# Score products of a local-attention block: 32 of 128 rows with zero-padded queries in place of 64 row-tile ones, and Exp's table loaded at another place

## What is computed

```
def local_attention(q, k, v):              # 16 heads of 64, windows of 32
    bk2, bv2 = (look(bk), look(bv))        # own window and the one before
    sim = jnp.einsum('bhwie,bhwje->bhwij', bq, bk2) * QK_SCALE
    sim = jnp.where(mask, -jnp.finfo(sim.dtype).max, sim)
    attn = jax.nn.softmax(sim, -1)
    out = jnp.einsum('bhwij,bhwje->bhwie', attn, bv2)

for i in range(6):
    x = attn_layer(shift_tokens(x), ...) + x     # q, k: l2norm, scale, rotary
    x = ffn_layer(shift_tokens(x), ...) + x      # layernorm, a * gelu(gate)

x = x + 0.5 * stack(layernorm(x))
x = x + recurrence(layernorm(x))
x = x + 0.5 * stack(layernorm(x))
```

## Time and profile before

| | |
|---|---|
| median of 3 runs | 3353.95 us (3350.72 to 3357.08) |
| the profiled execution | 3356.96 us, span 3355.2 us |
| granted TensorE clock | 0.996 of full speed |
| busy | PE 97%, PEld 74%, DVE 82%, ACT 76%, POOL 66% |
| steps | 192 tiles, one row maximum (L997) each |

### The profile page before, as it was taken

The page is one execution under the profiler, slowest core; times in us unless marked ns, Lnnn a source line. Parts: engine busy times, 40 slices in busy tenths (PEclk is TensorE's granted clock), DMA queues, the critical chain, the costliest instruction groups (busy, mean ns, idle before and its releaser), DMA issues. The chain is left out here.

```text
span 3355.2 us, 150147 instructions
## 1 busy us (share of the span) xinstructions
PE 3267.4 (97%) x63272; PEld 2487.9 (74%) x63464; DVE 2756.8 (82%) x6951; ACT 2542.9 (76%) x4144; POOL 2225.8 (66%) x1453
## 2 busy tenths in 40 slices
PE   7999999999999999999999999999999999999998
PEld 4777777777777777777777777777777777777776
DVE  7888888888878888889999888788888888888885
ACT  3777777777777777777777777777777777777775
POOL 6666666666666666667887666666666666666663
PEclk9999999999999999999999999999999999999999
DMA  3111111111111111111111111111111111111111
GB/s 122 44 47 44 47 44 47 44 46 44 40 47 44 47 44 47 44 47 45 38 47 43 48 44 45 41 44 47 44 47 44 47 44 44 44 41 47 47 52 38
DMA packets 135089, 157.39 MB, mean 47 GB/s; under 512 B 75539, under 2 KB 108439, under 8 KB 134423
## 3 DMA queue, kind: packets, MB, share of 16 engines
q1 hardware_dynamic: 129815, 144.42, 15.6%
q10 hardware_dynamic: 4608, 3.34, 0.3%
HBM read 33.38 MB, written 1.05 MB: 10 GB/s over the span
## 5 line engine op out<-in xcount | busy, mean ns | idle before, releaser
L1073 POOL TENSOR_TENSOR rot<-rot,swp 128x1024 f32<-128x1024 f32 x384 | 906.6, 2361 | 133.8 <-DVE rot L866 133.8
L673 ACT ACTIVATE sq<-proj 128x512 f32<-128x512 f32 x768 | 437.7, 596 | 459.5 <-PE proj L482 448.9
L482 PE MATMUL proj<-wq,xsT 128*128 128x512 f32 x1536 | 768.7, 622 | 14.3 <-DVE rot L866 11.1
L1082 POOL TENSOR_TENSOR rot<-rot,rn 128x1024 f32<-128x1024 f32 x384 | 724.1, 1907 | 0.0
L1063 POOL TENSOR_TENSOR rt<-rt,half 128x1 f32<-128x1 f32 x192 | 105.3, 548 | 797.4 <-DVE rt L936 797.4
L860 DVE TENSOR_TENSOR swp<-proj,tab 128x512 f32<-128x512 f32 x768 | 521.1, 679 | 5.7 <-ACT sq L673 3.6
L866 DVE TENSOR_TENSOR rot<-proj,tab 128x512 f32<-128x512 f32 x768 | 517.6, 674 | 0.6 <-PE tps L493 0.6
L493 PEld LDWEIGHTS tps<-idf,rot 128*128 128x128 f32 x3072 | 359.7, 141 | 204.3 <-issue 202.5
L990 DVE SCALAR_TENSOR_TENSOR hT<-proj,cols,fg 114x128 f32<-114x128 f32 (+1 forms) x576 | 166.7, 345 | 416.9 <-ACT fg L739 412.8
L1067 POOL TENSOR_TENSOR prob<-prob,rr 128x1024 f32<-128x1024 f32 x192 | 365.4, 1903 | 175.3 <-DVE rr L948 175.3
L525 PEld LDWEIGHTS sps<-kT,qT 64*32 64x32 f32 x24576 | 365.4, 107 | 130.0 <-issue 129.6
(11 more groups left out here) (102 smaller groups left out, 5872.1 us busy)
## 6 DMA issues: line engine op xcount, KB each, us to landing
vb<-va SPq DMA_DIRECT2D x192, 384.0 KB, 3.5
vb<-va SPq DMA_DIRECT2D x192, 128.0 KB, 3.6
wq<-in_L_ffn_Wqkv SPq DMA_DIRECT2D x95, 192.0 KB, 3.4
xs<-Z SPq DMA_DIRECT2D x192, 32.0 KB
wo<-in_L_ffn_Wo SPq DMA_DIRECT2D x94, 64.0 KB, 2.8
xs<-Z SPq DMA_DIRECT2D x192, 28.0 KB
xs<-Z SPq DMA_DIRECT2D x192, 3.8 KB
xs<-Z SPq DMA_DIRECT2D x192, 0.2 KB
```

The source lines that it names most:

```text
L482: mm(proj[:, c % 2, :], xsT[:, k.parity(L_QKV), 0:P], wq2[:, bass.ds(w + c * 512, 512)], start=True, stop=True).then_inc(p_qkv[c], 1)
L673: fn(sq[:, c * 512:(c + 1) * 512], proj[:, c % 2, :], ACT.Square).then_inc(a_sq[c], 1)
L1073: g_.tensor_tensor(r, r, swp[:, g * INNER:(g + 1) * INNER], ALU.add).then_inc(g_add[g], 1)
L1082: g_.tensor_tensor(r, r, rn[:, g * HEADS:(g + 1) * HEADS].unsqueeze(2) .to_broadcast([P, HEADS, DH]), ALU.mult).then_inc(g_nm[g], 1)
```

## The change

The queries get zeros. `qT` becomes, for each head pair and each of the 4 windows of the tile, two blocks of 32 columns: in block hp only the 64 rows of head hp hold queries, the other 64 rows are zero (set once by a memset on VectorE at the start). One product with all 128 rows, 64 columns of weights (two heads of 32 queries) and 64 moving columns of `kT` (both heads' keys on the rows) gives both heads' scores, since the zeros cancel the other head's keys. So there is one product where there were two, 32 in place of 64, and consecutive ones write to the other half of the output partitions (g).

The copy into `qT` becomes two, one for each head's 64 rows, since each goes to its own block. And ScalarE gets at the end of its step, after the xsT copies, an Exp on one column whose result `spare` nobody reads; the compiler's table load for Exp goes ahead of it, and Exp itself has none any more.

```
-        qT = sb("qT", [PAIRS, P])
+        qT = sb("qT", [PAIRS, POS // 2, 2, WIN])
...
+        spare = sb("spare", [1])
...
                 for p in range(PAIRS):
-                    for g in range(2):
-                        for hp, ty in ((0, 0), (1, 1), (0, 1), (1, 0)):
+                    for ty in range(2):
+                        for g in range(2):
                             w = 2 * ty + g
                             at = par * P + w * WIN
-                            rows = slice(hp * DH, (hp + 1) * DH)
-                            to = g * 64 + hp * WIN
-                            last = mm(sps[to:to + WIN, ty, p * 64:p * 64 + 64], qT[rows, p, w * WIN:(w + 1) * WIN],
-                                      kT[rows, p, at:at + 2 * WIN], start=False, stop=True, skip_group_check=True)
+                            last = mm(sps[g * 64:(g + 1) * 64, ty, p * 64:p * 64 + 64], qT[:, p, w, :, :].rearrange("p h i -> p (h i)"),
+                                      kT[:, p, at:at + 2 * WIN], start=False, stop=True, skip_group_check=True)
...
-                    cp(qT[:, :, :], tps[:, :, :]).then_inc(a_qT, 1)
+                    for hp in range(2):
+                        rows = slice(hp * DH, (hp + 1) * DH)
+                        last = cp(qT[rows, :, :, hp, :], tps[rows, :, :].rearrange("p c (w i) -> p c w i", i=WIN))
+                    last.then_inc(a_qT, 1)
...
+                if k.on(L_SM + 1) or k.on(L_S):
+                    fn(spare[:, :], half[:, 0:1], ACT.Exp)
...
+            v.memset(qT[:, :, :, :, :], 0.0)
```

## The result

| | before | after |
|---|---|---|
| median of 4 runs | 3355.14 us (3350.72 to 3357.08) | 3308.14 us (3307.57 to 3308.93) |
| the profiled execution | 3356.96 us, span 3355.2 us | 3308.44 us, span 3306.6 us |
| granted TensorE clock | 0.996 | 0.996 |

The ratio is 0.9862, with a 95% interval from 0.9845 to 0.9879: the changed kernel is 47 us faster.

A forecast was written before the change was run, and what follows sets the result against it. It took a loop VectorE, TensorE, ScalarE, TensorE, VectorE, with the scores last, as the bound. 3357.0 us - 49 (gaps) + 1 (middle stage) - 2 (pauses elsewhere) = 3307, less 3 for the median: 3304 us; range 3285 to 3325, chance 0.58.

The forecast's parts named there:

- The block stays as long: TensorE's scores: 64 load and matmul pairs at 28 ns replace 128 at 14.2 ns, 1.8 us a block as before.
- All 49 us of gaps go: Inside TensorE's scores: the 63 gaps beyond the usual pause ahead of each block, 49.0 us together, vanish.
- They reach L997: At VectorE's row maximum: the removed gaps shorten its wait for the scores almost fully, to near 60 us.
- The cause of the gaps: TensorE's scores: it runs through an instruction packet, some 250 instructions, in 1.8 us before the next is there.
- ScalarE: The second qT copy adds 1.0 us; Exp's 1.28 us table load moves into 1.68 us idle at step end; no cost.
- (a): Rival at TensorE's scores: the block gets shorter, 1.72 us or less; likely 3265 to 3285 us, floor 3245; chance 0.07.
- (b): Rival at TensorE's scores: the gaps stay or move to the attention product L540; 3350 us; chance 0.12.
- (c): Rival at TensorE's scores: a common feed makes a pair 38 ns, a block 2.4 us; +109 us, 3413 us; chance 0.10.
- (d): Rival at TensorE's scores: column groups take turns or loads aren't hidden, 3.6 us a block; +335 us, 3639 us; chance 0.08.
- (e): Rival on ScalarE: copies of 1.3 us or a tighter table place, 0.1 to 0.3 us a step; 3325 to 3360; chance 0.05.
- TensorE had stood 0.57 us for it: At the value products L488: TensorE waited 0.57 us for VectorE's rotation, so the step's loop runs through that rotation.
- That 0.25 us is all that faster scores could give: At the row maximum L997: VectorE stands 0.25 us more for scores after hT; its whole wait is 109.1 us.

The follow-up runs named there:

- split block: Kernel before, its 64 row-tile score products split into two halves of 32 with the second group of hidden products between them: 3379.1 us, ratio 1.0068.
- half-and-half block: Changed kernel with padded score products for head pairs 0 to 3 and old row-tile products for 4 to 7: 3336.2 us, ratio 0.9949.
- rotations first: Changed kernel with VectorE's two rotations of chunk 2 ahead of the reciprocal root's first steps: 3305.3 us; with half of the scores 3219.2 us.
- half of the output projection: Changed kernel with 4 of the 8 output projection products left out: 3306.0 us.
- half of the scores: Kernel before with only 32 of its 64 row-tile score products, the others left out: 3226.8 us, ratio 0.9624.
- both edits: Changed kernel with rotations first and half of the output projection left out: 3281.5 us, ratio 0.9786; with half of the scores 3200.7 us.

## Why the prediction held, and where it did not

The forecast of 3304 us was 4 us low. Of these 4 us, 1 is the runs of the kernel before, whose median came out at 3355 us. The forecast was right by the steps that carry it:

- *The block stays as long.* Right: 29 ns a pair where 28 was forecast, 1.8 us from first to last load. From the first load to the row maximum it came out 0.04 us longer. In 176 steps that would be 7 us, which the sum had not booked; it does not show in the total, since 48.2 us of gaps went and 48.6 us of time.
- *All 49 us of gaps go.* Right: 81.4 us in 192 gaps are left, the usual one ahead of each block and no other. L540's pauses took no part (35.9 before, 33.2 us after).
- *They reach L997.* Right: its wait is 60.5 us, forecast near 60.
- *The cause of the gaps.* The split block (49 to 21), the half-and-half block (to nearly 0 with 64 old loads left) and the old products in the changed kernel (back to 43) say that what counts is how many instructions stand together in a short time, and not the tile form. The count over the trace shows that it is a packet of the instruction queue: the estimate of some 250 instructions is 256, and every gap stands at a packet's border. With the gaps goes the spread, as it seems: the kernel before ran between 3347.9 and 3364.5 us in all comparisons, the changed one between 3307.6 and 3308.9 in its four runs.
- *ScalarE.* Right: two copies of 1.0 us, the table in the idle place, the squares' wait down to 0.23 us, no one late. The cost without the idle place came out higher than its expectation: 3463 us, and not 3440, for the padded products alone.
- *The rivals.* (a), shorter scores, fell at 29 ns. (b), gaps that stay, fell at 81.4 us. (c), a common feed of 38 ns a pair, fell by the same 29 ns. (d) was real in mechanism and did not strike, since g is the innermost loop: without this order it costs 317 us, forecast 335. (e) needed copies of over 1.3 us or a tighter place for the table; the copies cost 1.0 us, and the place had 0.23 us left.

In the Trainium skill, "TensorE: Matmul & The Clock Gate", section "The mechanism" of Part 3 has a load hidden only when its row group differs. The changed kernel speaks against it a second time. All its pairs use all rows, and two of them, side by side on the two halves, pass in 57 ns, where load and matmul one behind the other would take 114. Without the turns between the halves one pair takes 55 ns, also half of that.

Wrong was the step "TensorE had stood 0.57 us for it", by which the loop of the step was said to go through VectorE's last rotation. It was read off a weight load's wait. That wait lay under a running matmul, and the matmul row has 3.3 us of such waits in the whole span. The short steps are bound by TensorE's unbroken stream and by VectorE's rotation at once, within 0.1 us, and the long ones, every second, by the third path as it is read here. It did not matter for the forecast, since the scores come behind all of them. It did for the forecast made from it: rotations first came out 67 us above. The theories that I put in its place missed as well: TensorE's stream alone by 77 us (half of the output projection), two loops close together by 45 (rotations first with half of the scores), the tie of two by 20 and 26 (both edits, without and with half of the scores).

Off in size was "That 0.25 us is all that faster scores could give". Wait and overlap go together: where the wait of 0.30 us goes, VectorE's next operation also starts 0.09 us ahead of the other's end. Half of the scores gave 127 us, not 109, and so rival (a) had its floor of 3245 us too high: that kernel ran in 3227.

## What to carry to other kernels

Small products on TensorE cost instructions besides array time, and a dense block of them can run out of instructions although the array could go on: here 256 in 1.8 us did in a third of the steps. Count the loads and matmuls that stand together, and where zero-padding to full rows halves them at the same array time, as here, it can pay, as long as consecutive products write to different column halves and the engine that must copy into the padded form has the time. And before an engine's wait is put on the loop, look whether it is the weight load's or the matmul's, and shorten two ways together where single edits give nothing.

## What the runs showed of the hardware that I had not expected

- TensorE's instructions come in packets of 256, 64 bytes each, and all 63 gaps inside the scores stand at a packet's border.
- A block of small products changes its tile form at a price: 0.14 us between the old scores and a hidden product, 0.15 us a step between padded and old scores.
- Two loads and matmuls of full rows and 64 columns run side by side only when they go to different column halves in turn: 29 ns a pair in turn, 55 ns with the same products in another order.
- VectorE starts an operation 0.08 to 0.09 us before the one ahead of it ends. So a wait costs 0.09 us more than the profile's idle time shows. Where the kernel lets an operation wait for the one just ahead of it, the overlap is gone, and it starts 0.03 us after the other's end. With the rotations first, two more such places stand in each step, and VectorE is busy 2798.2 us in place of 2758.6, though its operations together are only 4 us longer.
- An Exp of one column more on ScalarE, in an idle place, came with 9 us more gaps in the old kernel's scores (69 in place of 63), but with 61 gaps where the qT copies were changed too. This stays open.
